# Second layer of a four-layer kernel: every operation placed by its own table entry, spread banks handed over in pairs, scan operands held as half batches

## The chip, the cores and the metric

The kernel runs on one core of a Trainium2 chip. The metric is the device time of one execution in microseconds. A core has five engines with a queue each: TensorE (PE), VectorE (DVE), ScalarE (ACT), GpSimd (POOL) and SyncE (SP, which here issues the transfers). Each works its own instructions strictly in order, and they wait for each other through semaphores.

## The reference

Four layers run one after the other over 8 batches of 256 positions (L) and 512 channels (E). The change touches the second one alone, a recurrent block in float32 with 32 heads of 16 channels:

```
xa  = layernorm(x);  sx = shifted(xa) - xa
xxx = tanh((xa + sx*maa_x) @ maa_w1)              # 5 groups of 32
xxx = einsum('blfd,fde->blfe', xxx, maa_w2)       # "mixes", 5 per batch
x_j = xa + sx * (maa_stack[j] + xxx[j])           # j = k, w, v, r, g
w   = exp(-exp(time_decay + tanh(xw @ td_w1) @ td_w2))
r, k, v = xr @ Wr.T, xk @ Wk.T, xv @ Wv.T;  g = silu(xg @ Wg.T)
step:  a = k v^T;  out = r . (u*a + s);  s = a + w*s     # 256 steps
og  = groupnorm(out) * gn_w + gn_b
x1  = x + (og*g) @ Wo.T
xc  = layernorm(x1);  sx2 = shifted(xc) - xc
out = x1 + sigmoid((xc + sx2*mr) @ Wfr.T) * (square(relu((xc + sx2*mk) @ Wfk.T)) @ Wfv.T)
```

The first layer is attention with an instance norm, the third two cross attentions and an MLP, the fourth a non-local block. They are the same in both kernels.

## The kernel before

The second layer is `layer1`. Tiles hold channels on 128 partitions and the 256 positions along the free axis, so a batch is four chunks of 128 channels (`EC` = 4). The recurrence is done by VectorE's scan instruction, which runs along the positions: one scan covers one index i of the 16x16 state of the 8 heads of a chunk. A batch has 4 chunks x 16 indices = 64 scans (`STEPS`), told as 16 quads of four. For each quad

- PE copies v to the rows that need it, with 0/1 matrices (`spread`, L1006, four matmuls of 256 columns, into PSUM banks 0 to 3);
- DVE multiplies that by k in place (`multiply`, L1421), and runs four scans (`scan_step`, L1434), which read the PSUM banks and write `SB`;
- POOL multiplies the states by r (L1394);
- PE sums them over i (`gather`, L1017), and DVE takes the sums after every fourth quad (`take_sums`, L1443).

Beside the scan of batch b the engines do the pre-stage of batch b+1 (`pre_stage`: layernorm, the hidden tanh, five mixes L1066, the projections k, r, v, g and the small decay projection) and the post-stage of batch b-1 (`post_stage`: group norm, Wo, layernorm, Wfk, Wfr, Wfv). So there are 10 rounds: one with a pre-stage alone, one of scan and pre-stage, six full ones, one of scan and post-stage, and a post-stage alone. A projection is `project` (L1029), half of a weight at a time: 8 float32 matmuls of 128x128 by 256 columns, which the profile lists as 16 instructions. All of the pre-stage's projections go through one PSUM bank (PA), all mixes through another (PF), and all of the post-stage through a third (PB), so each next one waits until DVE or ACT has read the last.

The order is written by hand. Each engine runs the same loop over n = 0 .. 63 (one n for each scan), and constants such as `AT_K`, `AT_V`, `MIX_AT` say at which n an operation is issued. An engine that reads the result has it at n+1 or n+2. Lines that matter below:

```
PE   spread(q+1) at n = 4q, waits s_ready of quad q-1 (all four scans)
DVE  multiply(q+1) at n = 4q+3, scan n at n
PE   gather(q-1) at n = 4q+2;  POOL weighs quad q at n = 4q+3
MIX_AT = (19, 25, 30, 37, 44)
AT_K, AT_R, AT_TW1, AT_TW2, AT_BONUS, AT_V, AT_G = 26, 33, 38, 40, 43, 47, 55
AT_GM, AT_GV, AT_BB, AT_WO, AT_MEAN, AT_VAR, AT_FK, AT_FR, AT_FV = 4, 10, 14, 22, 28, 32, 43, 51, 59
```

k, r, the decay w and the spread operand of v (`KT`, `RT`, `WT`, `VX`) are held twice, a whole batch each. `SB` is a ring of three quads.

Of the kernel before, what the change touches and what calls it, by code (L numbers as in the profile page):

```python
# [832 lines left out]
NV1 = 16  # L833
W_K, W_V, W_R, W_G, W_O, W_FK, W_FR, W_FV = range(8)
# [4 lines left out]
def layer1(nc, x1T, prevs, s0, vecs, w8, maa_w1, maa_w2, td_w1, td_w2, selv, selg, blk, bmc, bb, x2T):  # L839
# [5 lines left out]
    with ExitStack() as stack:  # L845
# [13 lines left out]
        STEPS = EC * S1  # L859
        HC1 = 8  # L860
        NH1 = EC * HC1

        W = sb("w", [P, 8, EC, E])
# [9 lines left out]
        BB = sb("bb", [NH1, EC, P])  # L873
# [14 lines left out]
        T1 = sb("t1", [DM, L])  # L888
        TW = sb("tw", [DD, L])
        KT = sb("kt", [P, 2, EC, L])  # L890
        RT = sb("rt", [P, 2, EC, L])
        WT = sb("wt", [P, 2, EC, L])
# [9 lines left out]
        RS = sb("rs", [NH1, L])  # L902
# [12 lines left out]
        def spread_bank(quad, s):  # L915
            return SPREAD + 2 * (quad % 2) + s // 2
# [16 lines left out]
        PA_MEAN, PA_VAR, PA_H0, PA_H1 = 1, 5, 16, 17  # L933
        MIX_AT = (19, 25, 30, 37, 44)
        AT_K, AT_R, AT_TW1, AT_TW2, AT_BONUS, AT_V, AT_G = 26, 33, 38, 40, 43, 47, 55
        AT_GM, AT_GV, AT_BB, AT_WO, AT_MEAN, AT_VAR, AT_FK, AT_FR, AT_FV = 4, 10, 14, 22, 28, 32, 43, 51, 59
# [5 lines left out]
        def stages(b):  # L942
            return (b if 0 <= b < B else None), (b + 1 if b + 1 < B else None), (b - 1 if b >= 1 else None)

        def at(n, first, count, every=1):

            i, r = divmod(n - first, every)
            return i if r == 0 and 0 <= i < count else None

        def mix_at(n, lag):  # L950

            for e, first in enumerate(MIX_AT):
                for i in range(2):
                    if n == first + 2 * i + lag:
                        return e, i
            return None

        @block.sync
        def _(sp):
# [1812 lines left out]
```

## Time and profile before

| | us |
|---|---|
| median of 3 runs | 4860.99 (4860.78 to 4861.16) |
| the profiled execution, its own time | 4855.27 |
| its span, first to last instruction | 4853.4 |
| stretch of the second layer in it | 849 to 2132 |

The profile is of one execution. A window line of it gives the busy time of each engine in a stretch with the number of instructions, then the granted TensorE clock (1.00 is 2.4 GHz, 0.50 is 1.2 GHz). A timeline line gives start, length, engine, line, operation, tiles, shapes and count, and in brackets how long the engine stood idle before it and who released it. DVEq and ACTq are the queues' own steps (such as a drain), and PEld is the loading of weights beside the matmuls.

### The profile page before, as it was taken

What the parts mean: (1) busy time and instruction counts of PE and PEld (TensorE: products, weight loads), DVE (VectorE), ACT (ScalarE), POOL (GpSimd) and SP (SyncE); (2) the same over time, 40 slices, a digit from 0 to 9 for tenths busy, and PEclk for the clock granted to TensorE, in tenths of its full rate; (3) what the DMA queues carried; (4) which work ended last, traced back from release to release, by engine and by line L of the source; (5) the groups of instructions that cost most, each with busy time, mean ns of one, the idle gap of its engine ahead of it and who ended that gap; (6) DMA issues with size and microseconds to landing.
All of it is one profiled execution on the core that took longest, in us unless ns stands there. A gap on an engine that the chain in (4) does not pass through costs nothing. (4 is left out here: it accounts for less than half of the span.)

```text
span 4853.4 us, 72484 instructions
## 1 busy us (share of the span) xinstructions
PE 4370.4 (90%) x22864; PEld 3258.0 (67%) x22864; DVE 3015.7 (62%) x6446; ACT 1930.0 (40%) x3756; POOL 1666.4 (34%) x1127
## 2 busy tenths in 40 slices
PE   6999997678888888659999999999999999999987
PEld 3444443456666666448878788797797877878864
DVE  5666663266676666627677577675675766757642
ACT  2555554112222222115555245453354542545511
POOL 1223323244444444312333433334323234333330
PEclk8999999779889899779999999999999999999999
DMA  1000000200000000012221222222312222221123
GB/s 37 23 27 18 27 18 10 99 9 1 14 14 14 14 10 9 9 60 65 67 70 59 70 90 64 73 66 64 97 60 74 62 66 92 62 70 54 62 69 115
DMA packets 126288, 240.89 MB, mean 50 GB/s; under 512 B 16884, under 2 KB 38132, under 8 KB 124896
## 3 DMA queue, kind: packets, MB, share of 16 engines
q1 hardware_dynamic: 123744, 229.50, 14.8%
q0 software_dynamic: 2304, 8.39, 0.4%
q8 instruction: 126, 2.06, 0.2%
q14 instruction: 114, 0.93, 0.1%
HBM read 220.79 MB, written 16.78 MB: 49 GB/s over the span
## 5 line engine op out<-in xcount | busy, mean ns | idle before, releaser
L1829 POOL TENSOR_TENSOR c_wl<-c_wr,c_wh 128x512 fp32r<-128x512 f32 (+1 forms) x576 | 823.6, 1442 | 1672.8 <-ACT c_wh L2141 1465.0
L1394 POOL TENSOR_TENSOR b_sb<-b_sb,b_rt 128x1024 f32<-128x1024 f32 x128 | 285.3, 2229 | 489.5 <-DVE b_sb L1434 489.5
L2235 ACT ACTIVATE c_pr<-c_ps,c_nms 128x257 f32<-128x257 f32 x512 | 244.4, 477 | 479.3 <-DVE c_nms L2429 476.9
L583 ACT ACTIVATE a_ex<-a_ps 128x1024 f32<-128x1024 f32 x256 | 261.4, 1024 | 260.2 <-PE a_ps L419 260.1
L1434 DVE TENSOR_TENSOR_SCAN b_sb<-b_wt,b_s,b_ps 128x256 f32<-128x256 f32 x512 | 355.8, 731 | 11.7 <-issue 4.4
L683 DVE TENSOR_REDUCE a_nm<-a_ps 128x2 f32<-128x1024 f32 x256 | 311.5, 1221 | 80.8 <-PE a_ps L396 80.7
L1888 PE MATMUL c_ps<-c_hh,c_wh 128*128 128x512 f32 x768 | 317.7, 414 | 34.1 <-POOL c_hl L1835 33.9
L1888 PE MATMUL c_ps<-c_gh,c_wh 128*128 128x512 f32 x768 | 307.5, 400 | 21.1 <-DVE c_gl L2467 17.4
L2141 ACT ACTIVATE c_wh<-c_wr 128x512 fp32r<-128x512 f32 (+1 forms) x464 | 316.4, 688 | 8.7 <-PE c_ps L1890 7.5
L1888 PE MATMUL c_ps<-c_wh,c_cth 128*128 128x256 f32 x1024 | 304.5, 297 | 9.3 <-DVE c_ctl L2382 5.0
L1890 PE MATMUL c_ps<-c_hh,c_wl 128*128 128x512 f32 x768 | 310.3, 404 | 0.0
L1889 PE MATMUL c_ps<-c_hl,c_wh 128*128 128x512 f32 x768 | 309.5, 403 | 0.0
L1890 PE MATMUL c_ps<-c_gh,c_wl 128*128 128x512 f32 x768 | 303.2, 395 | 0.0
L1889 PE MATMUL c_ps<-c_gl,c_wh 128*128 128x512 f32 x768 | 302.8, 394 | 0.0
L1029 PE MATMUL b_ps<-b_xf,b_w 128*128 128x256 f32 x1024 | 266.1, 418 | 38.7 <-DVEq L1480 29.7
L1890 PE MATMUL c_ps<-c_wh,c_ctl 128*128 128x256 f32 x1024 | 290.6, 284 | 0.0
L1889 PE MATMUL c_ps<-c_wl,c_cth 128*128 128x256 f32 x1024 | 289.7, 283 | 0.0
L433 PE MATMUL a_ps<-a_ex,a_vf 128*64 128x512 f32 x1024 | 278.9, 623 | 8.9 <-ACT a_ex L583 7.9
L1029 PEld LDWEIGHTS b_ps<-b_xf,b_w 128*128 128x128 f32 x1024 | 210.3, 210 | 91.6 <-issue 44.2
L2427 DVE TENSOR_REDUCE c_nm<-c_ps 128x1 f32<-128x257 f32 x512 | 215.1, 420 | 69.1 <-PE c_ps L1890 67.8
L2467 DVE TENSOR_TENSOR c_gl<-c_g,c_gh 128x512 fp32r<-128x512 f32 x128 | 95.3, 751 | 201.5 <-ACT c_gh L2222 201.5
L2423 DVE TENSOR_SCALAR c_pr<-c_pr,c_rs 128x257 f32<-128x257 f32 x512 | 184.7, 361 | 40.7 <-issue 1.3
(306 smaller groups left out, 10872.6 us busy)
## 6 DMA issues: line engine op xcount, KB each, us to landing
c_wr<-in_downs SPq DMA_DIRECT2D x192, 256.0 KB, 2.6
c_wr<-in_wv SPq DMA_DIRECT2D x64, 512.0 KB, 3.8
c_wr<-in_wk SPq DMA_DIRECT2D x128, 256.0 KB, 2.8
c_wr<-in_wq SPq DMA_DIRECT2D x128, 256.0 KB, 2.6
c_wr<-in_fc SPq DMA_DIRECT2D x64, 256.0 KB, 2.8
b_w<-in_w SPq DMA_DIRECT2D x8, 1024.0 KB, 12.8
a_x<-in_x SPq DMA_DIRECT2D x8, 512.0 KB, 3.5
a_ctx<-in_ctx SPq DMA_DIRECT2D x8, 512.0 KB, 4.1
```

Source lines behind the costliest of these rows:

```text
L433: mm = pe.matmul(ps[64 * a:64 * a + VCOLS, BO, :], VF[:, k, g * HG + 2 * p + a, :], EX[:, n % 4, a, :], start=(k == 0), stop=(k == EC - 1) ...
L583: act.activation(EX[:, n % 4, :, :], ps[:, BT + 2 * (n % 2):BT + 2 * (n % 2) + 2, :], ACT.Exp).then_inc(ex_ready, 1)
L683: dve.tensor_reduce(NM[:, s, :].rearrange("p (h c) -> p h c", h=HG)[:, 2 * p:2 * p + 2, c:c + 1], ps[:, bank:bank + 2, :], AX.X, ALU.max, ...
L1029: mm = pe.matmul(half(bank, o), W[:, w, k, o * P:(o + 1) * P], src[:, k, :], start=(k == 0), stop=(k == EC - 1), skip_group_check=True)
L1394: pool.tensor_tensor(SB[:, quad % 3, :, 0:L], SB[:, quad % 3, :, 0:L], RT[:, scan % 2, q // 4, :].unsqueeze(1).broadcast_to([P, 4, L]), AL ...
L1434: mm = dve.tensor_tensor_scan(SB[:, quad % 3, r, 1:L + 1], WT[:, b % 2, c, :], half(spread_bank(quad, r), r), S0[:, b % 2, c, 4 * jq + r:4 ...
L1829: pool.tensor_tensor(piece(WL, slot), piece(WR, slot), piece(WH, slot), ALU.subtract).then_inc(piece_cut[slot], 1)
L1888: pe.matmul(out, sh, mh, start=start, stop=False, skip_group_check=True)
L1889: pe.matmul(out, sh, ml, start=False, stop=False, skip_group_check=True)
L1890: return pe.matmul(out, sl, mh, start=False, stop=stop, skip_group_check=True)
L2141: act.activation(piece(WH, slot), piece(WR, slot), ACT.Copy).then_inc(piece_high[slot], 1)
L2235: act.activation(PR[:, i, 0:L + 1], ps[:, BS + 1 - i % 2, 0:L + 1], ACT.Exp, bias=NMS[:, i:i + 1], scale=float(K2) ** -0.5, accum_out=RS[: ...
```

## The change

The loop over n with its constants goes. Each engine now runs one loop over slots, half scan steps (128 to a batch, from -161 to 8 x 128 + 292), and a table for each engine (`PE_AT`, `ACT_AT`, `POOL_AT`, `DVE_AT`) gives each operation its slot relative to the first scan of its batch. `due(slot, first)` gives the batch whose turn it is, so stages overlap without round borders, and each half of a projection, mix or norm has its own entry on each engine. A slot number orders an engine's own queue and is no time: nothing but semaphores ties one engine's slot to another's.

With it come four other edits:

- spreads are issued in pairs of scans, two matmuls each, on a ring of four banks; pair p waits for the scans of pair p-4, and DVE multiplies 128x512 at a time;
- `KT`, `RT`, `WT`, `VX` hold three half batches (two chunks each); the rk product and the decay are made by halves; `SB` is a ring of four quads;
- mixes read all 128 rows: `W2` is padded to 128 rows for each mix, one row holds maa_stack against a row of ones in `T0` or `T1`, and time_decay comes in by such a row too. DVE then reads a mix with one 128x512 multiply where it had two 128x256 instructions and a drain;
- `T0`, `T1`, `TW`, `RS` are filled once at the start by four memsets; the constant transfers grow (W2 from 128x2x512 to 128x5x512, TW2 from 64 to 128 rows, BB from 32 to 128 rows).

```diff
-        W2 = sb("w2", [P, 2, E])
+        W2 = sb("w2", [P, 5, E])
-        TW2 = sb("tw2", [DD, E])
+        TW2 = sb("tw2", [P, E])
-        BB = sb("bb", [NH1, EC, P])
+        BB = sb("bb", [P, EC, P])
-        KT = sb("kt", [P, 2, EC, L])
-        VX = sb("vx", [P, 2, 2, EC, L], F32R)
-        SB = sb("sb", [P, 3, 4, L + 1])
+        KT = sb("kt", [P, 3, 2, L])
+        VX = sb("vx", [P, 3, 2, 2, L], F32R)
+        SB = sb("sb", [P, RING, 4, L + 1])          # RING = 4
...
+        PE_AT = dict(spread=-14, gather=15, mean=-153, var=-121, hidden=-102, mix=(-95, -91, -89, -83, -81, -75, -62, -53, -44, -37), k=(-84, -82),
+                     r=(-67, -63), tw1=-62, tw2=(-52, -44), bonus=(-38, -37), v=(-33, -24), g=(-18, -9), gm=(143, 145), gv=151, bb=(156, 160),
+                     wo=(170, 177), mean2=185, var2=192, fk=(229, 233), fr=(249, 258), fv=(265, 268))
+        DVE_AT = dict(multiply=-1, sums=51, mean=-117, inverse=-108, blend=-99, mix=(-91, -89, -85, -72, -68, -63, -48, -42, -39, -32), v=(-24, -16),
+                      gm=(156, 157), ginverse=158, bb=(162, 163), wo=(185, 191), mean2=194, inverse2=206, fkin=227, frin=235, fv=(277, 282), out=284)
...
+        def due(slot, first):
+            t, r = divmod(slot - first, SLOTS)
+            return t if r == 0 and 0 <= t < B else None
...
-                if quad >= 2:
-                    pe.wait_ge(s_ready, quad - 1 + AHEAD)
+                if pair >= 4:
+                    pe.wait_ge(s_ready, pair - 3 + AHEAD)
                 for i in range(2):
-                    for a in range(2):
-                        mm = pe.matmul(half(spread_bank(quad, 2 * a), i), SELV[:, 2 * jq + i, :], VX[:, b % 2, a, c, :], ...)
+                    mm = pe.matmul(half(spread_bank(pair), i), SELV[:, 2 * jq + i, :], VX[:, third(b, c), a, c % 2, :], ...)
...
-                        mm = pe.matmul(half(PF, o), W2[strip, f // 4, o * P:(o + 1) * P], T0[strip, :] if f < 4 else T1[:, :], ...)
+                        mm = pe.matmul(half(PF, o), W2[:, f, o * P:(o + 1) * P], (T0 if f < 3 else T1)[:, :], ...)
...
-                    for o in range(2 * i, 2 * i + 2):
-                        mm = dve.scalar_tensor_tensor(XF[:, e % 2, o, :], half(PF, o), vec(V_STACK + MIXES[e], o), SXA[:, o, :], ALU.add, ALU.mult)
-                    dve.drain().then_inc(mix_read, 1)
+                            dve.tensor_tensor(XF[:, e % 2, pair, :], both(PF), SXA[:, pair, :], ALU.mult).then_inc(mix_read, 1)
...
-            for b in range(-1, B + 1):
-                scan, pre, post = stages(b)
-                for n in range(STEPS):
-                    q, r = divmod(n, 4)
-                    if scan is not None and r == 0 and q + 1 < QUADS:
-                        spread(scan, q + 1)
+            for slot in range(FIRST, LAST):
+                for pr in range(PAIRS1):
+                    b = due(slot, 4 * pr + PE_AT["spread"])
+                    if b is not None:
+                        spread(b, pr)
+                for q in range(QUADS):
+                    b = due(slot, 8 * q + PE_AT["gather"])
+                    if b is not None:
+                        gather(b, q)
+                post_stage(slot)
+                pre_stage(slot)
```

PE's queue of the kernel before, around the start of the group norm in a full round. vx,selv is a spread, sb,selg a gather, xpb,w is Wfv of the round's end, og,bm and sqb,bmc the group norm's two sums, rs,bb its way back, za,meanw the pre-stage's variance, za,w the hidden layer:

```order
L1029 MATMUL b_ps<-b_xpb,b_w 128x256 x16
L1017 MATMUL b_ps<-b_sb,b_selg 32x256 x4
L1006 MATMUL b_ps<-b_vx,b_selv 128x256 x8
L1038 MATMUL b_ps<-b_xa,b_meanw 128x256 x4
L1017 MATMUL b_ps<-b_sb,b_selg 32x256 x4
L1006 MATMUL b_ps<-b_vx,b_selv 128x256 x4
L1117 MATMUL b_ps<-b_og,b_bm 128x256 x2
L1043 MATMUL b_ps<-b_za,b_meanw 128x256 x4
L1017 MATMUL b_ps<-b_sb,b_selg 32x256 x4
L1117 MATMUL b_ps<-b_og,b_bm 128x256 x2
```

The same place in PE's queue of the changed kernel:

```order
L1040 MATMUL b_ps<-b_xpb,b_w 128x256 x8
L1017 MATMUL b_ps<-b_vx,b_selv 128x256 x2
L1040 MATMUL b_ps<-b_xpb,b_w 128x256 x8
L1017 MATMUL b_ps<-b_vx,b_selv 128x256 x2
L1028 MATMUL b_ps<-b_sb,b_selg 32x256 x4
L1131 MATMUL b_ps<-b_og,b_bm 128x256 x4
L1017 MATMUL b_ps<-b_vx,b_selv 128x256 x4
L1028 MATMUL b_ps<-b_sb,b_selg 32x256 x4
L1138 MATMUL b_ps<-b_sqb,b_bmc 32x256 x4
L1017 MATMUL b_ps<-b_vx,b_selv 128x256 x2
L1066 MATMUL b_ps<-b_za,b_w 96x256 x4
```

Wfv's two halves now have a spread between them and the group norm follows them directly; the next batch's mean has moved out of this place, half a round ahead.

DVE's queue of the kernel before, at the first two mixes and Wo. kt,ps is a multiply, wt,s,ps a scan, xf a mix read, xb a reading of Wo:

```order
L1467 SCALAR_TENSOR_TENSOR b_xf<-b_ps,b_vec,b_sxa 128x256 x2
L1434 SCALAR_TENSOR_TENSOR b_sb<-b_wt,b_s,b_ps 128x256 x2
L1467 SCALAR_TENSOR_TENSOR b_xf<-b_ps,b_vec,b_sxa 128x256 x2
L1421 TENSOR_TENSOR b_ps<-b_kt,b_ps 128x1024
L1434 SCALAR_TENSOR_TENSOR b_sb<-b_wt,b_s,b_ps 128x256
L1502 TENSOR_TENSOR b_xb<-b_xb,b_ps 128x512
L1434 SCALAR_TENSOR_TENSOR b_sb<-b_wt,b_s,b_ps 128x256 x2
L1502 TENSOR_TENSOR b_xb<-b_xb,b_ps 128x512
```

DVE's queue of the changed kernel, from the first mix on:

```order
L1521 TENSOR_TENSOR b_xf<-b_ps,b_sxa 128x512
L1482 SCALAR_TENSOR_TENSOR b_sb<-b_wt,b_s,b_ps 128x256
L1468 TENSOR_TENSOR b_ps<-b_kt,b_ps 128x512
L1521 TENSOR_TENSOR b_xf<-b_ps,b_sxa 128x512
L1482 SCALAR_TENSOR_TENSOR b_sb<-b_wt,b_s,b_ps 128x256 x2
L1468 TENSOR_TENSOR b_ps<-b_kt,b_ps 128x512
L1521 TENSOR_TENSOR b_xf<-b_ps,b_sxa 128x512
L1482 SCALAR_TENSOR_TENSOR b_sb<-b_wt,b_s,b_ps 128x256 x2
L1468 TENSOR_TENSOR b_ps<-b_kt,b_ps 128x512
L1482 SCALAR_TENSOR_TENSOR b_sb<-b_wt,b_s,b_ps 128x256 x2
```

A multiply now stands ahead of every two scans. The first reading of Wo, which stood one scan behind the second mix, now comes behind the third mix and seven more scans, past the rows shown.

## Rows read from the trace of the kernel before

**Rows 1.** Windows: the rounds; us, busy us (count) of five engines, PEclk, DMA share, GB/s.

```profile
849.00:957.00 108.00, 76.15 (x223) 53.48 (x224) 19.02 (x37) 15.77 (x28) 17.44 (x8) 0.70 0.28 107
959.50:1076.50 117.00, 87.23 (x401) 59.27 (x400) 79.75 (x114) 20.37 (x47) 54.67 (x26) 0.80 0.01 5
1219.60:1363.00 143.40, 124.33 (x587) 89.59 (x586) 97.16 (x137) 33.33 (x68) 65.06 (x30) 0.89 0.04 12
1936.30:2039.30 103.00, 72.30 (x352) 48.43 (x352) 76.85 (x105) 15.35 (x35) 42.26 (x20) 0.78 0.03 11
2039.30:2132.00 92.70, 54.20 (x176) 37.95 (x176) 15.21 (x21) 13.51 (x21) 8.56 (x4) 0.73 0.05 17
```

**Rows 2.** Timeline of PE at full clock, one group of matmuls behind the other.

```profile
1408.88 3.72 PE L1029 MATMUL b_ps<-b_zb,b_w 128*128 128x256 f32 x16 [0.38 <-DVE b_xb L1502]
1412.53 1.13 PE L1066 MATMUL b_ps<-b_t,b_w 32*128 32x256 f32 x4
1413.59 0.64 PE L1017 MATMUL b_ps<-b_sb,b_selg 128*32 128x256 f32 x8
1414.16 3.72 PE L1029 MATMUL b_ps<-b_xf,b_w 128*128 128x256 f32 x16
...
1426.33 0.72 PE L1006 MATMUL b_ps<-b_vx,b_selv 128*128 128x256 f32 x4
1426.89 1.89 PE L1152 MATMUL b_ps<-b_sqb,b_meanw 128*128 128x256 f32 x8
1428.71 1.12 PE L1066 MATMUL b_ps<-b_t,b_w 32*128 32x256 f32 x4
```

**Rows 3.** Windows of 10 us in one full round, columns as in rows 1.

```profile
1415.00:1425.00 10.00, 10.00 (x54) 7.95 (x52) 7.66 (x10) 0.89 (x3) 4.34 (x2) 1.00 0.00 0
1385.00:1395.00 10.00, 8.76 (x26) 5.40 (x27) 9.81 (x13) 0.32 (x1) 4.31 (x3) 0.52 0.00 0
1375.00:1385.00 10.00, 5.76 (x38) 2.94 (x36) 7.74 (x11) 4.46 (x11) 6.45 (x3) 0.99 0.01 2
```

**Rows 4.** Waits in the round 1219.6:1363: who waited for whom, us, times, longest.

```profile
DVE b_zb L1525 <- PE b_ps L1029: 8.8, 2, 6.2
PE b_ps L1006 <- DVE b_sb L1434: 7.5, 5, 3.6
PE b_ps L1029 <- DVEq L1480: 3.2, 1, 3.2
PE b_ps L1017 <- POOL b_sb L1394: 2.2, 2, 1.5
```

**Rows 5.** Groups by line in the same round: count, busy us, mean ns, idle before.

```profile
L1434 DVE TENSOR_TENSOR_SCAN b_sb<-b_wt,b_s,b_ps 128x256 f32<-128x256 f32 x64 | 44.7, 731 | 1.6 <-issue 0.6 <-DVE b_ps L1421 0.2
L1421 DVE TENSOR_TENSOR b_ps<-b_kt,b_ps 128x1024 f32<-128x1024 f32 x17 | 20.7, 1217 | 3.6 <-PE b_ps L1006 3.0
L1467 DVE SCALAR_TENSOR_TENSOR b_xf<-b_ps,b_vec,b_sxa 128x256 f32<-128x256 f32 x20 | 8.7, 477 | 12.6 <-PE b_ps L1066 12.6
```

**Rows 6.** Timeline of DVE and ACT: a 128x512 reading; start of the layer.

```profile
1408.14 0.69 DVE L1502 TENSOR_TENSOR b_xb<-b_xb,b_ps 128x512 f32<-128x512 f32 x1 [2.91 <-PE b_ps L1029]
...
861.40 0.47 ACT L1215 ACTIVATE b_sda<-b_ps,b_eps 128x256 f32<-128x256 f32 x1 [3.87 <-PE b_ps L1043]
861.54 0.69 DVE L1407 CAST b_selv<-b_zb 128x1024 fp32r<-128x1024 f32 x1 [5.19 <-DMA b_bb<-in_bb]
```

**Rows 7.** Timeline of PE: last projection ahead of the first spread; last gather, and what follows.

```profile
953.87 3.72 PE L1029 MATMUL b_ps<-b_xf,b_w 128*128 128x256 f32 x16 [1.26 <-ACTq L1271]
957.24 1.29 PE L1006 MATMUL b_ps<-b_vx,b_selv 128*128 128x256 f32 x8
...
2041.34 1.08 PE L1017 MATMUL b_ps<-b_sb,b_selg 128*32 128x256 f32 x8 [4.01 <-POOL b_sb L1394]
2042.35 2.08 PE L1117 MATMUL b_ps<-b_og,b_bm 128*128 128x256 f32 x4
```

**Rows 8.** Transfers in 840:900: GB/s in 40 slices of 1.5 us.

```profile
GB/s 350 0 0 0 5 25 314 227 346 298 314 393 374 358 393 426 426 426 421 410 426 421 431 421 418 361 62 0 0 0 0 0 0 0 0 0 0 0 0 11
```

More of the change, by code:

```diff
@@ L940, in layer1, with scan_at @@
         block = stack.enter_context(nc.Block())
[L942 to L956, printed above, removed]
+        def due(slot, first):
+            t, r = divmod(slot - first, SLOTS)
+            return t if r == 0 and 0 <= t < B else None
+        def scan_at(slot, lag=0):
+            return divmod(slot - lag, SLOTS)
         @block.sync
@@ L1044, in pre_stage @@
                     mm.then_inc(a_var, 1)
-                if n == PA_H0:
+                t = due(slot, PE_AT["hidden"])
+                if t is not None:
                     if t == 0:
@@ L1083, in pre_stage @@
-                if n == AT_TW1:
-                    u = t * UNITS + U_TW1
+                for e in range(5):
+                    for i in range(2):
+                        t = due(slot, PE_AT["mix"][2 * e + i])
+                        if t is not None:
+                            f = MIXES[e]
+                            if e == 0 and i == 0:
+                                pe.wait_ge(t_ready, t + 1 + AHEAD)
+                            else:
+                                pe.wait_ge(mix_read, t * 10 + e * 2 + i + AHEAD)
+                            for o in range(2 * i, 2 * i + 2):
+                                mm = pe.matmul(half(PF, o), W2[:, f, o * P:(o + 1) * P], (T0 if f < 3 else T1)[:, :], start=True, stop=True, skip_group_check=True)
+                            mm.then_inc(mix_ps, 1)
@@ new lines, in pre_stage @@
+                for i in range(2):
+                    t = due(slot, PE_AT["bonus"][i])
+                    if t is not None:
+                        pe.wait_ge(rk_ready, t * 2 + i + 1 + AHEAD)
+                        if t == 0 and i == 0:
+                            pe.wait_ge(bo_ready, 1 + AHEAD)
+                        before_pa(t * UNITS + U_BONUS + i)
+                        for c in range(2 * i, 2 * i + 2):
+                            mm = pe.matmul(half(PA, c), BO[:, c, :], ZA[:, c, :], start=True, stop=True, skip_group_check=True)
+                        mm.then_inc(pa_ps, 1)
@@ new lines, in post_stage @@
+            def post_stage(slot):
+                for i in range(2):
+                    s = due(slot, PE_AT["gm"][i])
+                    if s is not None:
+                        pe.wait_ge(og_ready, s * EC + 2 * i + 2 + AHEAD)
+                        if i == 0:
+                            pe.wait_ge(fv_read, s * 2 + AHEAD)
+                        else:
+                            pe.wait_ge(gc_ready, s * 2 + 1 + AHEAD)
+                        for c in range(2 * i, 2 * i + 2):
+                            mm = pe.matmul(half(PB, c), BM[:, :], OG[:, s % 2, c, :], start=True, stop=True, skip_group_check=True)
+                        mm.then_inc(gm_ps, 1)
+                s = due(slot, PE_AT["gv"])
+                if s is not None:
```

718 lines of the change are left out of this document (369 added, 349 removed).

## Prediction

> **What bounds the kernel now.** I read the windows by round first. The second layer is 849 to 2132 of the span, and six full rounds, from 1076.5 to 1936.3, make 859.8 us of it, 143.3 each [rows 1]. In one of them PE is busy 124.3 us, DVE 97.2, POOL 65.1, ACT 33.3, so no engine is full, and PE is nearest. The same row has PE's clock at 0.89: with two levels, 1.00 and 0.50, 22% of the round (31.5 us) ran at 1.2 GHz.
>
> Next the timeline of PE at full clock, for what the work costs back to back [rows 2]. Half a projection to the next group is 1412.53 - 1408.88 = 3.65 us, a pair of mix matmuls 1.06, a gather 0.57, a spread of four 0.56, a group of four matmuls (x8) 1.82. A full round holds 16 half projections (58.4 us), 8 groups of four (the two layernorms' means and variances, two hidden, the group norm's variance, the decay's first: 14.6), 18 pairs (10 mixes, 2 each of decay, bonus, group mean and its way back: 19.1), 16 gathers (9.1), 16 spreads (9.0). That is 110 us. So the round of 143.3 splits into 110 of work at full clock, 14 that the low clock adds (124.3 busy less 110), and 19 in which PE stands.
>
> Third, who lets PE stand, in the waits [rows 4]: 7.5 us on DVE's scans before spreads, 3.2 on DVE's reading of v, the rest small. And DVE in turn waits for PE: 12.6 us for mixes [rows 5] and 8.8 for Wfv [rows 4]. This mutual waiting is what an in-order pair of queues gives when the space between them is small. The windows of 10 us show the other half [rows 3]: where PE is full (10.00 of 10), the clock is 1.00 and the work flows; in 1375:1385 it is busy for 5.76, and in the next stretch the clock is 0.52.
>
> **The change part by part: how far apart PE and DVE may be.** Before, spread q+1 stands at n = 4q and is used by the multiply at n = 4q+3: three scan steps, six slots. After, a spread of pair p stands at slot 4p-14 and its multiply at 4p-1: 13 slots. It may be issued as soon as the scans of pair p-4 (slots 4p-16 and 4p-14) are done, so PE never leads DVE by slot number, and may lag by up to 13 slots (some 12 us), where a round of DVE's ran into PE's long projections after six. I followed one round through the two queues, with the times of [rows 2] for PE and those of [rows 5, 6] for DVE. It closes. From the group norm's first sum (PE slot 15) PE works through two sums, the hidden layer, two ways back, three mixes, Wo, Wk in some 26 us; DVE goes from slot 26 to about 55 beside it. PE is then 10 slots behind, which is what mix 4 (PE slot 47, needs DVE's slot 56) and Wo's second half (49, needs 57) want. Between 47 and 84 PE catches up to 3 behind, since the work there is thinner, and DVE waits for spreads; at 84 to 110 mixes 8 and 9 and v need 3 to 5. Over Wg, Wfr and Wfv (seven half projections and a variance, 29 us with its spreads and gathers) DVE runs ahead again to slot 26. The gaps I found on PE: 0.9 between the two group sums and 0.6 behind them, 0.7 between the first two mixes, 0.4 between the halves of Wfv, 0.4 before Wo, together 3.0; I take 4 for what a hand count misses.
>
> **The finer spreads.** 32 groups of two matmuls for 16 of four. No row shows a group of two. Without any loss they cost the same 9.0 us; at worst each takes as long as the group of four (0.56), which adds 32 x 0.56 - 9.0 = 8.9. A gather of eight instructions takes 0.57 and so shows no large cost for a group of its own; I take 0.34 each, +1.9.
>
> **DVE's own work.** Multiplies: 16 of 128x1024 at 1.217 are 19.5; 32 of 128x512 at the 0.69 of a same-sized reading [rows 6] are 22.1, +2.6. Mix reads: 20 x 0.477 = 9.5, less overlap 8.7 [rows 5], become 10 x 0.69 = 6.9, -1.8, and ten drains go. DVE stays at 98 us a round, which is under PE's. The Trainium skill (VectorE: DVE Perf Modes, The TRN2 errata) says that each VectorE instruction carries a fixed cost, and so to keep tiles at 512 elements or more. By that rule the halved multiply is a step back. The rows agree on the sign (2 x 0.69 over 1.217), and it does not reach the end while PE is the longer.
>
> **Mixes on 128 rows.** A matmul of a 32-row and of a 128-row operand took much the same here (1.06 us for four instructions, 3.65 for sixteen [rows 2], which is 0.27 and 0.23), so nothing; the bounds are -1 and +1, a tenth of the ten mixes' 10.6. ACT's decay has one exp of 128x512 for two of 128x256 each half: ACT is busy 33 of 143 [rows 1], which hides it. POOL's two half products of r and k instead of one add a start-up, hidden while POOL is at 65.
>
> **The clock.** With the gaps down from 19 to 4 us, PE would be busy 97% of the time. A full stretch had 1.00 [rows 3]. What remains of the low clock sits where the gaps are, at the group norm and first mixes, 2.2 us of idle in 20. I take a quarter of the 14 us, +3.5. Bounds: 0, and all 14.
>
> The full round is then 110 + 1.9 + 4 + 3.5 = 119.4; I round up to 120. Six of them: 6 x (143.3 - 120) = 140 us less.
>
> **The ends.** In the first scan's round (117 us, DVE busy 79.8, PE 87.2 [rows 1]) nothing is full either; PE's work there at full clock is 8 x 3.65 + 5 x 1.82 + 14 x 1.06 + 18.1 + 1.9 = 73, DVE's 80. It could fall to some 95 or stay at 117; I take 107, -10. In the last one (103, DVE 76.9) the wait for Wfv goes out of the round, but Wfv of batch 6 (slots 265 and 268 of its batch, so 137 and 140 of the last) then stands between the last gather (135) and the group norm. Before, the group norm follows the last gather directly [rows 7]. That costs the tail two half projections with their readings, 2 x (3.65 + 0.8) = 9, and the round before it gets shorter by about as much or slightly more: 0 for the two. At the start, W2, TW2 and BB grow by 768 + 128 + 192 KB. The transfers run at some 400 GB/s by then [rows 8], so the constants land 2.7 us later, and DVE takes them in ahead of the first inverse: it waited for them until 861.54 while the root was ready at 861.87 [rows 6], so nothing hides this, +2.7. Against it, the first spread now stands ahead of Wg's second half (3.4 us before the spread at 957.24 [rows 7]): -3.4. Four memsets on POOL are under a microsecond. Ends together -10.
>
> Sum: 4855.3 - 140 - 10 = 4705 for an execution like the profiled one. The median of the runs is 5.7 above that one: 4711. I round to 4710.
>
> **Rivals.**
> *The clock stays low* (21%). The change cuts the spreads into more and shorter groups with a semaphore wait each, and puts two short waits a round at the group norm. Were the clock at 0.89 as now, a round would be 110 + 1.9 + 4 + 14 = 130: 6 x 13.3 = 80 less, and 8 at the ends, gives 4855.3 - 88 + 5.7 = 4773. For it speaks that in 1375:1385 the many short groups (38 instructions) came with idle time, and the low clock behind them [rows 3]; against it that the full stretch has the full clock in the same rows. The Trainium skill (TensorE: Matmul & The Clock Gate, A second HAM failure mode: psum-queue depth-cycling) describes just this: frequent micro-idles while PSUM banks are cycled make the clock swing between its two levels. By that rule the time is this rival's.
>
> *The slot tables don't fit the engines* (10%): POOL (POOL's mixes, weighing and norms share one queue) or ACT is late in places, each releasing PE some 1.5 us late at six to ten places a round, gaps of 15 instead of 4 and a clock as now: 110 + 1.9 + 15 + 14 = 141 a round, 4855.3 - 14 - 5 + 5.7 = 4842. For it speaks that gathers wait for POOL already [rows 4]; against it that POOL is busy for 65 us only [rows 1].
>
> *Slower* (4%). The group norm's first sum on PE (slot 15) waits for DVE's second reading of Wfv (slot 26), and DVE can be at 26 only if it is at the very end of the lead that the spreads of slot 14 allow. If DVE comes there late, PE stands while DVE walks up to 11 slots at 98/128 = 0.77 us, 8.4 us; the same at slots 17, 47 and 49. With all four missed the round is 120 + 34 = 154, +64 over six, so 4855.3 + 64 + 5.7 = 4925. It decides from about three misses a round (23.4 us). Against it: 29 us of PE's work lie ahead of that place and DVE has only about 26 of its own there.
>
> The rest, 65%, is the forecast. Its own range: with full clock and 3 us of gaps 115 a round and ends -18, 4855.3 - 170 - 18 + 5.7 = 4673; with finer spreads at +8.9, 126.4 and ends -5, 4855.3 - 101 - 5 + 5.7 = 4755. The range over all cases, 4665 to 4790, leaves out the second rival and the last, 14%. A difference of 0.2%, 10 us, is about what a measurement can tell from none. Faster by more than that: 65 + 21 and most of the second rival, 0.94. Within it 0.02, slower 0.04.
>
> **What would show it.** In the changed profile a full round between output stores takes about 120 us, with PE busy 114 to 117 and a clock above 0.95; DVE is busy 98, 82%. DVE's multiply waits for spreads, and PE's spreads hardly wait for scans (under 2 us a round for 7.5). PE's gaps are at the group norm. A pair of spread matmuls starts some 0.34 before the next group. The constants' copy comes near 864. I am wrong if the round is above 127, if the clock is still 0.89, or if DVE or POOL fill the round; and the hand-followed round is wrong if PE waits more than 2 us at any one place.

## The result and the profile after

The changed kernel took 4616.98 us (median of 4 runs, 4615.37 to 4623.2), the kernel before 4860.89 in the same job. The ratio is 0.9501, with a 95% interval of 0.9485 to 0.9518: 244 us faster, where 151 were forecast. The direction and the place were right. The gain was forecast too small, and the time lies below the stated range. The profiled execution of the changed kernel took 4615.37.

The windows by round answer to [rows 1]: the start of the layer, the first scan's round, one full round, the last round, the tail.

```profile
851.00:943.40 92.40, 60.00 (x220) 44.32 (x220) 17.87 (x28) 15.44 (x27) 17.63 (x9) 0.79 0.35 137
943.40:1040.30 96.90, 76.34 (x400) 55.61 (x400) 78.77 (x121) 20.15 (x47) 54.98 (x26) 0.88 0.02 6
1285.80:1395.70 109.90, 106.49 (x586) 82.90 (x584) 94.03 (x143) 33.17 (x67) 63.75 (x30) 1.00 0.05 16
1700.60:1809.40 108.80, 87.51 (x452) 62.37 (x450) 81.38 (x124) 17.68 (x41) 47.75 (x22) 0.87 0.03 10
1809.40:1889.30 79.90, 47.76 (x161) 34.83 (x160) 14.10 (x19) 13.52 (x21) 6.57 (x3) 0.79 0.04 14
```

From the second full round on, a round takes 110.0 us for 143.3. PE is busy 106.5 of them at a clock of 1.00, and idle for 3.4. The first full round is another one. It also lasts 110.4 us, with less work in it (no Wfv falls there yet), PE idle for 12.6 and the clock at 0.95:

```profile
1040.30:1150.70 110.40, 97.83 (x535) 74.45 (x528) 91.57 (x140) 32.21 (x65) 63.75 (x30) 0.95 0.03 11
```

The whole of the change lies in the layer:

| Phase | Before | After | Difference | Forecast |
|---|---|---|---|---|
| First load to first scan | 111.7 | 92.9 | -18.8 | -0.7 |
| First scan's round | 117.0 | 96.9 | -20.1 | -10 |
| Six full rounds | 859.8 | 660.3 | -199.5 | -140 |
| Last round and tail, to the last store | 192.3 | 188.7 | -3.6 | 0 |
| First load itself (847.9, then 850.6) | | | +2.7 | |

The sum is -239.3. The two profiled executions differ by 239.9. The first load comes 2.7 later because the layer ahead of it ends that much later in this execution (GpSimd's first memset of the second layer stands at 846.09 for 843.40), so that is not the change's.

PE's timeline at full clock answers to [rows 2].

```profile
1302.29 3.62 PE L1040 MATMUL b_ps<-b_zb,b_w 128*128 128x256 f32 x16
1305.74 3.62 PE L1040 MATMUL b_ps<-b_xf,b_w 128*128 128x256 f32 x16
1309.20 1.03 PE L1080 MATMUL b_ps<-b_t,b_w 128*128 128x256 f32 x4
1309.87 0.58 PE L1017 MATMUL b_ps<-b_vx,b_selv 128*128 128x256 f32 x2
1310.29 3.61 PE L1040 MATMUL b_ps<-b_xf,b_w 128*128 128x256 f32 x16
```

From start to start, half a projection costs 3.45 us before a projection or a mix, where it was 3.65 before a mix. A mix costs 0.67 before a spread (0.97 before a projection), where it was 1.06. The spread of two shown costs 0.42.

PE's waits in the same round answer to [rows 4], and these five are all that it has.

```profile
PE b_ps L1080 <- DVE b_xf L1521: 0.9, 1, 0.9
PE b_ps L1131 <- DVE b_og L1540: 0.9, 1, 0.9
PE b_ps L1138 <- ACT b_sqb L1309: 0.8, 1, 0.8
PE b_ps L1040 <- DVE b_zb L1586: 0.5, 1, 0.5
PE b_ps L1017 <- DVE b_sb L1482: 0.2, 1, 0.2
```

Spreads wait 0.2 us for scans, where it was 7.5. The first full round has two long ones, beside 1.3 us of short ones:

```profile
PE b_ps L1056 <- ACT b_za L1229: 6.7, 1, 6.7
PE b_ps L1131 <- DVE b_og L1540: 4.6, 1, 4.6
```

The groups by line answer to [rows 5], here of 1284.9 to 1394.8.

```profile
L1482 DVE TENSOR_TENSOR_SCAN b_sb<-b_wt,b_s,b_ps 128x256 f32<-128x256 f32 x64 | 45.4, 736 | 1.5 <-DVE b_ps L1468 0.2
L1468 DVE TENSOR_TENSOR b_ps<-b_kt,b_ps 128x512 f32<-128x512 f32 x32 | 21.7, 678 | 5.8 <-PE b_ps L1017 5.8
L1017 PE MATMUL b_ps<-b_vx,b_selv 128*128 128x256 f32 x64 | 16.6, 350 | 0.2 <-DVE b_sb L1482 0.2
L1080 PE MATMUL b_ps<-b_t,b_w 128*128 128x256 f32 x40 | 10.6, 387 | 0.9 <-DVE b_xf L1521 0.9
```

DVE and ACT at the layer's start [rows 6] read so now: the root is ready at 864.03 + 0.47, the constants' copy runs at 866.52, and the first inverse stands behind it. Behind the first load the copy is at 16.0 us for 13.7.

```profile
864.03 0.47 ACT L1233 ACTIVATE b_sda<-b_ps,b_eps 128x256 f32<-128x256 f32 x1 [3.87 <-PE b_ps L1056]
866.52 0.69 DVE L1455 CAST b_selv<-b_zb 128x1024 fp32r<-128x1024 f32 x1 [7.54 <-DMA b_bb<-in_bb]
868.12 1.75 DVE L1505 RECIPROCAL b_sda<-b_sda 128x256 f32<-128x256 f32 x1
```

PE ahead of the first scan answers to [rows 7]. The first spreads now stand before Wg's second half, and a half projection behind 3.56 us of idle time takes 6.41 for 3.72, most of it at half the clock.

```profile
935.86 6.41 PE L1040 MATMUL b_ps<-b_xf,b_w 128*128 128x256 f32 x16 [3.56 <-DVEq L1533]
941.92 0.82 PE L1017 MATMUL b_ps<-b_vx,b_selv 128*128 128x256 f32 x4
943.52 3.72 PE L1040 MATMUL b_ps<-b_xf,b_w 128*128 128x256 f32 x16 [0.79 <-ACTq L1301]
```

### The profile page after: what moved, and what is told of

It reads as the page before. It is cut to its first block and busy times, and to the rows that moved or that the text cites. A ratio compares the mean times of both kernels' runs of the same rounds, so it can differ in the third digit from the quotient of the medians.

```text
span 4613.7 us, 72508 instructions
## 1 busy us (share of the span) xinstructions
PE 4238.2 (92%) x22864; PEld 3208.3 (70%) x22864; DVE 2998.3 (65%) x6494; ACT 1928.3 (42%) x3748; POOL 1659.0 (36%) x1139
## 3 DMA queue, kind: packets, MB, share of 16 engines
q8 instruction: 127, 2.08, 0.2%
## 5 line engine op out<-in xcount | busy, mean ns | idle before, releaser
L1040 PE MATMUL b_ps<-b_xf,b_w 128*128 128x256 f32 x1024 | 238.2, 386 | 13.0 <-DVEq L1533 9.1
L1040 PEld LDWEIGHTS b_ps<-b_xf,b_w 128*128 128x128 f32 x1024 | 194.0, 193 | 48.2 <-issue 17.9
```

Of the source, the lines that this page charges most:

```text
L1040: mm = pe.matmul(half(bank, o), W[:, w, k, o * P:(o + 1) * P], src[:, k, :], start=(k == 0), stop=(k == EC - 1), skip_group_check=True)
```

## The experiments

All times are medians. "Against the change" is against 4617.0, or against 4615.5, the changed kernel run beside them (e14), for those marked *. e13, e16 and e17 are built on e8.

| Run | us | Ratio to before | 95% interval | Against the change |
|---|---|---|---|---|
| e1_narrow_mix | 4655.3 | 0.9567 | 0.9538 to 0.9596 | +38 |
| e3_ring3 | 4671.8 | 0.9599 | 0.9570 to 0.9629 | +55 |
| e6_narrow_all | 4666.7 | 0.9599 | 0.9585 to 0.9614 | +50 |
| e5_placement | 4759.7 | 0.9807 | 0.9772 to 0.9842 | +143 |
| e12_all | 4718.3 | 0.9719 | 0.9692 to 0.9745 | +101 |
| e12_mix | 4689.2 | 0.9637 | 0.9612 to 0.9662 | +72 |
| e10_g_first | 4622.2 | 0.9508 | 0.9492 to 0.9524 | +5 |
| e14_after_again | 4615.5 | 0.9497 | 0.9484 to 0.9510 | |
| e8_constants_late | 4612.7 | 0.9492 | 0.9479 to 0.9505 | -3* |
| e13_swaps | 4646.9 | 0.9556 | 0.9543 to 0.9569 | +31* |
| e16_gm_apart | 4611.7 | 0.9477 | 0.9457 to 0.9498 | -5 |
| e17_both | 4624.3 | 0.9502 | 0.9481 to 0.9522 | +7 |
| e4b_before_wide_both | 4816.5 | 0.9897 | 0.9868 to 0.9927 | |
| e4_before_wide_pe | 4826.4 | 0.9922 | 0.9896 to 0.9948 | |
| e9_before_pairs | 4975.7 | 1.0225 | 1.0194 to 1.0255 | |
| e11_before_pairs_wide | 4929.7 | 1.0137 | 1.0120 to 1.0154 | |

**The mixes' rows.** In e1 only the mixes read 32 rows:

```
-  mm = pe.matmul(half(PF, o), W2[:, f, ...], (T0 if f < 3 else T1)[:, :], ...)
+  mm = pe.matmul(half(PF, o), W2[32*(f%3):32*(f%3)+32, f, ...], (T0 if f < 3 else T1)[32*(f%3):32*(f%3)+32, :], ...)
```

> The changed kernel, but the ten mixes a round read 32 rows again (the row of maa_stack is left out of the product). Theory A: a group of matmuls on 32 rows does not overlap with its neighbours on 128 rows, so each mix costs PE some 0.2 us ahead and 0.2 to 0.35 behind it; 4 to 5 us a round, seven rounds with mixes, +30 to +35 us: about 4650, a full round near 114.5 instead of 110.0. If the gaps also bring the low clock back, up to +60. Theory B: the row count changes nothing, as the prediction had it, and placement gave all of it: 4617 within 10.

It came out at +38. The windows of a round, and of its first mixes:

```profile
1282.16:1397.55 115.39, 112.53 (x586) 84.46 (x585) 94.63 (x143) 33.17 (x67) 63.76 (x30) 0.97 0.04 15
...
1300.00:1310.00 10.00, 8.22 (x50) 5.74 (x50) 8.51 (x15) 3.23 (x6) 5.25 (x3) 1.00 0.16 58
1322.20:1332.20 10.00, 10.00 (x35) 7.80 (x32) 9.28 (x15) 0.00 (x0) 7.70 (x4) 0.66 0.00 0
```

The round is 5.4 us longer and the way to the first scan 3.6. PE is busy 6.0 us longer. Some 3.4 of these are the 10 us at 0.66 behind the first mixes, a dip that the changed kernel lacks (1.00 from its second full round on). The rest, 2.6, is what the ten groups and those ahead of them take more from start to start. Of four rounds between output stores three are like this one, and one has a clock of 0.99 and takes 113.9.

The same was put into the kernel before: in e4b with both parts, in e4 with the matmuls alone and DVE's reading of two halves and a drain kept. Groups then sum over what other mixes hold, and the output differs for that.

```
-  pe.matmul(half(PF, o), W2[strip, f // 4, ...], T0[strip, :] if f < 4 else T1[:, :], ...)
+  pe.matmul(half(PF, o), W2[:, f // 4, ...], (T0 if f < 4 else T1)[:, :], ...)
```

> The kernel before with two edits: the mix matmuls take all 128 rows (of the same operands, so the four groups are summed, and the mixes are not the reference's), and DVE reads a pair of them with one 128x512 multiply, without maa_stack and the drain. Theory A (overlap of neighbouring matmuls): PE's work falls by 4 to 5 us a round, the round by 3 to 6, and the low clock may shrink: 4815 to 4840. Theory B: nothing on PE, only DVE's shorter reading, under 1.5 us a round: 4850 to 4861.

> The kernel before with the mixes' matmuls on all 128 rows, and DVE's reading as it was (two instructions of 128x256 with maa_stack, and a drain). Groups then sum over what other mixes hold; the output differs for that. With DVE's reading widened as well it took 4816.5, ratio 0.9897, -46 against the 4862.5 of before. Theory A (the PE part: 32-row groups do not overlap with their neighbours, 1.06 for 0.67 to 0.9 us): 4818 to 4828, nearly all of it. Theory B (the DVE part: the read is 0.95 plus a drain before and 0.69 after, and PE waits for the bank): 4845 to 4860, PE busy as before, 124.

They took 46 and 34 us less than before. One window of the round of each, e4b first:

```profile
1205.70:1345.60 139.90, 119.98 (x584) 88.91 (x584) 94.94 (x127) 33.31 (x68) 64.80 (x29) 0.90 0.04 12
```

```profile
1207.00:1346.90 139.90, 119.79 (x586) 88.84 (x585) 97.15 (x137) 33.31 (x68) 64.84 (x30) 0.90 0.04 12
```

PE is busy 4.4 and 4.5 us less than in [rows 1], and the round is 3.5 shorter in both. From first load to last store the layer takes 1243.5 us in e4b and 1244.9 in e4, for 1280.7. So the matmuls carry nearly all of it, and DVE's shorter reading little. Six rounds of 3.5 are 21 us; the rest lies at the layer's ends.

**All narrow groups, and the fourth set of scan outputs.** In e6 the decay and the way back are narrow too. In e3 the change is kept but for `RING = 3`. e5 is both.

> The changed kernel with SB as a ring of three quads as before. Theory A: PE runs up to ten slots behind DVE, so the gather of quad q-3 can come after the scan of quad q is due, and DVE waits: +1 to +3 us a round, 4625 to 4640. Theory B: three are enough, 4617 within 5.

> The changed kernel with the slot tables, the ring of four pairs and the half-batch buffers kept, but with all 14 groups (mixes, decay, the group norm's way back) on 32 or 64 rows (the two added rows are left out, so maa_stack and time_decay are not added), and with three sets of scan outputs. Theory A (gains add): the narrow mixes' +38 us and the third set's +55 us, measured one by one, add, with some 8 for decay and way back: 4615 + 38 + 55 + 8 = 4716, round about 125. Theory B (they overlap: with three sets PE stands anyway, so what a narrow group costs it is partly hidden): 4675 to 4695, round 118 to 121. Theory C (placement brings little, the rest was buffers and rows): above 4780.

> The changed kernel with all 14 groups of mixes, decay and way back on 32 or 64 rows (without the added rows of maa_stack and time_decay), and its four sets of scan outputs kept. It is the kernel with three sets that took 4759.7 (ratio 0.9807) with the fourth set put back. Theory A (decay and way back cost what four more narrow groups cost, 4 of 10 times the mixes' 38): 4617 + 38 + 15 = 4670, round 116 to 117, and the fourth set is then worth 90 in this kernel for 55 alone, since each takes away slack that the other needs. Theory B (decay and way back sit on the path of the group norm and are what costs): 4700 to 4720, round 120 or more.

In e3 DVE's scan waits for the gather that frees the oldest set:

```profile
DVE b_sb L1482 <- PE b_ps L1028: 14.3, 7, 5.4
```

The kind was foreseen, and the size (+55) was not. e6 came out as theory A of its expectation has it. e5 came out between its theories, above A and B and under C: 143 is more than 50 and 55 together. With everything narrow the fourth set is worth 93. A round of e5 from store to store has 7.8 us of idle time on PE, about what e3 has with wide groups, but 124.5 of busy time for e3's 108.6 and a clock of 0.87 for 0.98. The round, and two stretches out of it:

```profile
1347.20:1479.50 132.30, 124.47 (x584) 90.43 (x583) 94.39 (x142) 33.15 (x67) 63.74 (x30) 0.87 0.04 13
...
1360.90:1365.90 5.00, 5.00 (x18) 2.48 (x17) 3.23 (x6) 0.14 (x1) 4.76 (x3) 0.50 0.00 0
1415.90:1420.90 5.00, 5.00 (x19) 2.48 (x18) 3.67 (x6) 1.33 (x3) 4.16 (x2) 0.50 0.00 0
```

Its four rounds between stores last 129 to 132 us, at 0.87 to 0.90. With 26% of 132.3 us at half the clock PE loses 17 of them, more than the waits cost. The low clock is where the two losses meet. The tables with the ring of pairs, the buffers and DVE's shorter reading of a mix, without the rows and the fourth set, bring 100 of the 244 us.

**The ring of pairs in the old order.** e9 is the kernel before with two matmuls a spread and four pairs in the ring. e11 adds the wide mixes.

```
-                first = spread_bank(quad, 0)
...
+                a = both(SPREAD + pair % 4)
```

> The kernel before with the pair ring alone: a spread of two matmuls for each pair at n = 2p-7, waiting for the scans of pair p-4, its multiply ahead of scan 2p. Nothing else is moved. Theory A: the distance between spread and multiply (13 half steps for 6) is what lets both queues run: PE's 7.5 us of waiting for scans and part of DVE's for mixes go, 8 us a round and more, 4770 to 4810. Theory B: the placement of the other operations is what counts, and the pairs alone give less than 2 us a round: 4847 to 4865.

> The kernel before with the ring of four pairs (alone 4975.7, ratio 1.0225) and with the mixes on 128 rows (alone 4816.5, ratio 0.9897; maa_stack is added twice in a sense, since groups on all 128 rows sum over what other mixes hold; the output differs for that). Theory A (what 128 rows save, PE's overlap with its neighbours and ten short DVE instructions, is on the path in any order of the program): both effects add, ratio 1.0225 x 0.9897 = 1.012, 4921. Theory B (with the ring in the old order each engine mostly waits for the other, so cheaper groups are hidden): 4955 to 4980.

e9 lost 113 us, which neither theory had. Its waits in one round:

```profile
PE b_ps L1006 <- DVE b_sb L1434: 27.9, 13, 4.6
DVE b_xf L1467 <- PE b_ps L1066: 17.2, 8, 5.9
DVE b_zb L1525 <- PE b_ps L1029: 15.2, 2, 12.5
```

Each engine waits for the other longer than in [rows 4] and [rows 5]: PE 27.9 us for scans (7.5 before), DVE 17.2 for mixes (12.6) and 15.2 for Wfv (8.8). The readings stand right behind what PE makes, so DVE stops at them, and the spread behind it lacks its scans. But e9 changed a second thing. Before, the spread at n = 4q asks for scans up to n = 4q-1, and PE is free up to n = 4q+4. In e9 every second n has a spread that asks for the scan of the same n, so PE can no longer run ahead of DVE there. How much of the 113 is that and how much the place of the readings, no run separates. e11's 1.0137 is the product of the two ratios (1.0120) within the intervals.

**Where the readings stand.** In e12_all five of DVE's ten readings of mixes (the halves 3 to 7, counted from 0) stand 7 or 8 slots behind PE's slot, for 11 to 14, and those of Wo and Wfv 5 slots, for 12 to 15. In e12_mix only the mixes are moved.

```
-  DVE_AT mix=(-91, -89, -85, -72, -68, -63, -48, -42, -39, -32), wo=(185, 191), fv=(277, 282)
+  DVE_AT mix=(-91, -89, -85, -76, -73, -67, -54, -46, -39, -32), wo=(175, 182), fv=(270, 273)
```

> The changed kernel with only DVE's readings of PE's results moved: mixes 3 to 7, Wo and Wfv are read 4 to 10 slots after the PE slot that makes them, for 9 to 15. Theory A (the space between writer and reader is what the table gives: DVE is 0.8 us a slot, PE lags by up to 12 slots): DVE comes to the reading before PE has made the result, waits, and PE then lacks scans: the round goes from 110.0 to 116 to 124, time 4655 to 4700, with DVE waiting over 6 us a round more for PE at mixes, Wo or Wfv. Theory B (DVE has 16 us of slack a round, so where it reads does not matter): within 8 us of 4617.

> The changed kernel with only the readings of mixes 3 to 7 moved 4 to 8 slots earlier, with Wo's and Wfv's left in place. All moved together took 4718.3 (ratio 0.9719), 101 more. Theory A (space is needed everywhere alike; the mixes are five of nine moved readings): 4655 to 4680. Theory B (what costs is Wfv's reading ahead of the last gathers and the group norm, where the trace has gaps of 3.84 and 2.12 us on PE): 4617 to 4640.

Both lost more than either theory had. One place in a round of e12_mix shows how, on DVE and then on PE:

```profile
1218.32 0.69 DVE L1521 TENSOR_TENSOR b_xf<-b_ps,b_sxa 128x512 f32<-128x512 f32 x1 [3.45 <-PE b_ps L1080]
1218.92 0.74 DVE L1482 TENSOR_TENSOR_SCAN b_sb<-b_wt,b_s,b_ps 128x256 f32<-128x256 f32 x1
1219.58 0.66 DVE L1559 TENSOR_TENSOR b_xb<-b_xb,b_ps 128x512 f32<-128x512 f32 x1
```

```profile
1220.29 5.41 PE L1040 MATMUL b_ps<-b_zb,b_w 128*128 128x256 f32 x16 [2.08 <-DVE b_xb L1559]
```

DVE stops 3.45 us at a mix that PE has not made, and so comes late to Wo's first half, whose reading was not moved. PE waits for it. Behind the gap Wo's second half takes 5.41 for 3.73, in part at the low clock. DVE has 16 us of slack a round and still sets the time by where it stands.

**The start.** e10 puts Wg's second half back ahead of the first spread (`g=(-18, -9)` to `g=(-18, -15)`). e8 moves the constants' reading behind DVE's first blend.

> The changed kernel with Wg's second half at slot -15 for -9, that is ahead of the batch's first spread as it was before. Theory A (the start term as forecast): the layer's first scan comes 3.3 us later and the full rounds stay within 0.5 us of 110.0, in all +3 to +6. Theory B (the half projection was cover for DVE's last readings of v): each round loses 1 us or more, +9 or more. Theory C: no difference at the start, since the first scan waits for DVE's v and its decay, not for PE.

> The changed kernel with the first batch's readings of the constants moved behind DVE's first blend, so that the first inverse does not wait for the 1088 KB that the change adds to them. Theory A (the constants' copy holds up the layer's first batch): -2 to -4 us against the changed kernel in the same job. Theory B (PE waits there for its weights or for other things anyway): within 1 us.

> The changed kernel as it is, on the same chip as the two that follow, to compare them with: 4617, ratio 0.950, within 0.15% either way.

In e10 the first scan starts 97.4 us behind the layer's first load (854.6 to 952.1), for 92.9, but the layer ends only 0.9 later (1039.6 from first load to last store, for 1038.7). What the first scan gains is mostly given back before the first store (326.1 us from the first load in e10, 325.3 in the changed kernel). e10's full rounds then take 110.8 for 110.0, with one wait more (0.71 us on ACT, before a half projection), and the last stretches give that back. In e8 DVE takes the inverse first:

```profile
887.36 1.75 DVE L1503 RECIPROCAL b_sda<-b_sda 128x256 f32<-128x256 f32 x1 [5.56 <-ACT b_sda L1233]
895.76 1.67 DVE L1509 SCALAR_TENSOR_TENSOR b_za<-b_sxa,b_vec,b_xpa 128x256 f32<-128x256 f32 x4 [6.65 <-POOL b_sxa L1390]
897.56 0.69 DVE L1455 CAST b_selv<-b_zb 128x1024 fp32r<-128x1024 f32 x1
```

Its layer lasts 1035.0, or 3.6 less than in e14, as theory A has it. The first scan comes 89.2 to 89.5 us behind the first load in e8, e13 and e17, for 92.9 and 92.6 in two executions of the changed kernel. The medians differ by 2.8, which their intervals don't tell apart. (In the profiled executions of e8, e14 and e16 the work ahead of the layer took some 19 to 23 us longer. Only times within the layer are compared with them.)

**Closing the last gaps.** e13 moves the next batch's variance between Wfv's halves (`var=-121` to `-117`) and the first mix ahead of the second way back. e16 and e17 instead set the group norm's second sum a spread later (`gm=(143, 145)` to `(143, 147)`). e17 also reads Wfv's first half earlier (`fv=(277, 282)` to `(275, 282)`). All three have the constants late.

> The kernel of the constants' late reading, with two moves at the gaps of 0.9 and 0.55 us a round that the changed kernel's PE still has: the variance of the next batch's first layernorm stands between Wfv's halves (slot -117 for -121), and the first mix stands ahead of the group norm's second way back (PE -97 for -95, DVE's reading -94 for -91). Theory A (both gaps go, PE is the bound): 1.2 to 1.5 us a round less, with the constants 10 to 13 us less than the changed kernel, about 4605. Theory B (the gaps move to the next place, since ACT's and DVE's chain behind the group norm sets them): 0 to 4 less than the changed kernel.

> The changed kernel with the constants read late, and with the group norm's second sum on PE at slot 147 for 145, so that a spread stands between the two and covers some 0.35 of the 0.87 us in which PE waits for DVE's first reading. Theory A: 0.3 us a round less than with the constants late alone, 4612.7 - 2 = 4610 to 4612. Theory B (ACT's squares and the variance behind it come that much later, as when the first mix was moved, and the gap opens there): 4613 to 4620.

> As the last one, and DVE reads Wfv's first half at slot 275 for 277, ahead of one multiply, one scan more, so that PE's 0.55 us between Wfv's halves goes. Theory A: 0.8 us a round less than with the constants late alone, 4607 to 4609. Theory B: DVE then waits there for PE's first half, PE's next spread comes late, and nothing is won or up to 15 lost: 4613 to 4628.

e13 lost 31 us against the change, and 34 against e8, on which it is built. A round of it on PE, and then on DVE:

```profile
1312.62 0.51 PE L1017 MATMUL b_ps<-b_vx,b_selv 128*128 128x256 f32 x2 [1.36 <-DVE b_sb L1482]
...
1399.98 1.89 PE L1056 MATMUL b_ps<-b_za,b_meanw 128*128 128x256 f32 x8
1404.77 5.41 PE L1040 MATMUL b_ps<-b_xpb,b_w 128*128 128x256 f32 x16 [2.90 <-DVE b_zb L1586]
```

```profile
1402.41 1.75 DVE L1503 RECIPROCAL b_sda<-b_sda 128x256 f32<-128x256 f32 x1 [3.08 <-ACT b_sda L1233]
1404.09 0.63 DVE L1586 SCALAR_TENSOR_TENSOR b_zb<-b_sxb,b_ps 128x512 f32<-128x512 f32 x1
```

The variance came later, so DVE's inverse waited 3.08 us for its root. Wfv's reading stands behind it in the queue, and PE's second half waited 2.90 for that bank and ran in part at half the clock. All five rounds between 1150 and 1750 have this. A gap of 0.55 had become one of 2.90 plus 1.7 of slow work. The first mix's gap of 0.93 came back as 1.36 before the spread.

e16 leaves the round at 110.0: the gap between the sums fell from 0.87 to 0.64, and the one before the group norm's variance grew from 0.83 to 1.06. Its median is the lowest of all, 5 us under the change and 1 under e8, but the intervals of the ratios overlap, so it isn't shown to be the better. Its profiled layer is 5.9 us shorter than e8's, but 2.8 of that lie ahead of the first scan, where the two programs are the same, so single layers differ by that much without a cause in the program. e17 lost 13 against e16: at the group norm of a round PE waits for ACT, and in some rounds works slowly behind it. Two rounds one after the other:

```profile
1177.26 3.36 PE L1138 MATMUL b_ps<-b_sqb,b_bmc 128*32 128x256 f32 x8 [2.29 <-ACT b_sqb L1309]
...
1291.07 1.91 PE L1138 MATMUL b_ps<-b_sqb,b_bmc 128*32 128x256 f32 x8 [2.29 <-ACT b_sqb L1309]
```

## Where the prediction was too small, and what held

The steps that failed are two terms of the round and the sum of the ends. Mixes on 128 rows were put at nothing, and narrow ones cost e1 5.4 us a round (2.6 of work, the rest low clock). What remains of the low clock was put at +3.5, and is 0 from the second full round on. The ends were put at -10 and gave -42.5. The round came out at 110.0 for the 120 forecast, which is 60 of the missing 93 us. These 10 us a round are 3.5 for the clock, some 5.4 by which PE's work was put too high (about half of it the rows), 0.6 of gaps and 0.6 of rounding up.

**Right: the space between the engines.** "PE never leads DVE by slot number, and may lag by up to 13 slots" holds. From the second full round on, spreads wait 0.2 us for scans, PE's idle time is 3.4 where 4 was taken, and it stands where the hand count had it: 0.87 between the group sums (0.9) and 0.83 behind them (0.6), 0.93 between the first mixes (0.7), 0.55 between Wfv's halves (0.4). Before Wo there is none (0.4). In the first full round the waits of 6.7 and 4.6 us are over the 2 that the forecast named as the sign that its hand-followed round is wrong; its hand count was of a round with Wfv in it. e12 shows that the space between PE and DVE is needed (101 us when the readings of mixes, Wo and Wfv move closer, 72 with those of the mixes alone), and e3 that a fourth set of outputs is part of it. The forecast counted that set as given and never priced it. That the tables alone bring the gain no run shows: e5's 100 us are tables, ring of pairs, buffers and DVE's reading together.

**Failed: "Mixes on 128 rows ... so nothing; the bounds are -1 and +1".** I divided a group's time by its instructions (0.27 against 0.23) and took them for alike. The runs say 38 us in the new kernel (50 with all 14 groups, e6) and 34 to 46 in the old, 5.4 and 3.5 us a round and the rest at the ends, where the bounds allowed 1 a round. In the new kernel 2.6 of the 5.4 are the groups' own time and the rest the clock that falls with them. [Rows 2] held the sign of it: a half projection before a narrow mix was 3.65, where the same trace has 3.37 before a spread, and four matmuls cost 0.27 each for 0.23. The runs show the price and not its mechanism.

**Failed: "I take a quarter of the 14 us, +3.5".** The clock is 1.00 in five of the six full rounds, and 0.95 in the first. The bound of 0 was the truth there, and it depends on the term above: e1 and e6, with about the same gaps and narrow groups, mostly have 0.97. e5 has 0.87 to 0.90, and e3, with the idle time of e5 and wide groups, 0.96 to 0.98. The rival whose clock stays low was wrong for this kernel and near e5 in its number (4759.7; it gave 4773). The Trainium skill (TensorE: Matmul & The Clock Gate, A second HAM failure mode: psum-queue depth-cycling) has frequent micro-idles swing the clock. The changed kernel cycles four banks with groups of two and has five waits a round, and from its second full round on its clock stays at 1.00, so here the trace does not agree.

**PE's busy time, 106.5 for the forecast's 115.4.** From start to start in the timeline of 1284.8 to 1394.8: the clock's 3.5 is gone; the 16 half projections take 53.9 us for 58.4, since 3.65, the price ahead of a narrow mix, stood for all of them; the 18 pairs take 14.7 for 19.1 (the 14 wide ones 0.83 each for 1.06, and the four of bonus and group mean, which had 128 rows before, some 0.8 where 1.06 was taken too). Against that the 32 spreads take 13.7 for 10.9, and the gathers 9.5 for 9.1. That gives 106.2. So the rows are about half of the 5.4 us of work (2.6 by e1, 2.8 by e6, with the low clock taken off), and the rest is a sum at full clock that was too dear. The finer spreads (+1.9, bounds 0 to 8.9) cost 4.7 over the 9.0 taken for the old ones. DVE was 94 us for 98.

**The ends: "together -10", and -42.5 without the later first load (-18.8, -20.1 and -3.6).** Before the first scan the forecast had -3.4 and +2.7. Both were about right in size at their places (4.5 earlier by e10, 3.7 later by e8), though the first is worth 0.9 at the end of the layer. Missing was the rest: with all groups narrow (e6) the first scan stands 102.9 us behind the first load, for 92.9 with wide ones and 111.7 before, so 10 of the 18.8 are the rows once more. Most of these 10 are the clock: it is at 0.50 in e6 from 923.3 to 933.3, 70 us behind the first load, where the changed kernel and e1 have 1.00, and e1 loses only 3.6. With 4.5 for the earlier spread, and 3.7 the other way for the constants, some 8 stay open. In the first scan's round the 20 us were inside what I had named ("some 95 or stay at 117"), and I took the middle; what brings them no run shows. In the last round and tail 0 against -3.6 is near. There the group norm waits as the forecast said, since Wfv of batch 6 now stands before it.

**The rivals.** From the second full round on POOL is never late for PE (it is busy 63.8 of 110), and ACT once, by 0.8. In the first full round ACT is, by 6.7. Of the four misses at slots 15, 17, 47 and 49 only one at the group norm occurred, once, with 4.6 us in the first full round, for 8.4 taken. e13 and e17 show such a mechanism in every round: one late reading or sum at the group norm or at Wfv costs 12 to 34 us.

**Not tried:** the tables with the ring of quads, and the tables with whole-batch buffers. So what the ring of pairs and the half-batch buffers do in the new order is open.

## What to carry to other kernels

Where two in-order engines feed each other, try each reading some ten slots (half scan steps) behind what it reads, with rings that have as many slots of room. Readings 7 or 8 slots behind, for 11 to 14, lost 72 us here, and the ring in the old order lost 113. Keep the rows of all small matmul groups equal to their neighbours', even with zeros, and read a group's cost from start to start on both sides of it. Near a full engine, move a step only after following every instruction that is queued behind its readers: two moves meant to close gaps of 0.9 and 0.55 us cost 34. And look at the first full round by itself: here it has 12.6 us of idle time where the steady round has 3.4.

## What the runs showed of the hardware

A group of four fp32 matmul instructions on 32 rows costs 1.06 us from start to start and makes the projection ahead of it 0.2 longer (3.65 for 3.45). On 128 rows it costs 0.67 before a spread and 0.97 before a projection. The four times as many rows come for less than nothing.

Idle time alone does not tell where PE's clock falls. In e1 the stretch behind the narrow mixes ran at 0.66 with PE busy 10.00 of 10. The changed kernel kept 1.00 there, with more idle time in its round (3.4 us for 2.9). Its gaps of up to 0.93 us cost it no clock.

Nor does the size of a gap. Behind 2.90 us (e13) and 2.08 (e12_mix) half a projection took 5.41 for 3.73 in every round that has the gap. Behind e17's 2.29 the same group took 3.36 and 3.39 in two rounds and 1.91 in three, and behind e3's 2.25 another kept its 1.10 in four rounds of six:

```profile
1420.25 1.10 PE L1131 MATMUL b_ps<-b_og,b_bm 128*128 128x256 f32 x4 [2.25 <-DVE b_zb L1586]
```
